# One-hot tables of a top-2 expert router built with the batch's columns innermost, and read by the tensor engine in strides of eight elements

## The reference

```python
var = mean(x * x, axis=-1)
xn = rms_w * (x * rsqrt(var + 1e-6))
gate = xn @ wg_W + wg_b + (cond @ gg_W + gg_b)
cw = top-2 weights of softmax(gate), zero for the other six experts
h1 = relu(x @ W1[e] + b1[e])
h2 = relu(h1 @ W2[e] + b2[e])
out = x + sum over e of cw[e] * (h2 @ W3[e] + b3[e])
```

## Time and profile before

| | |
|---|---|
| runs of the kernel before, us | 550.54, 550.29, 549.07; median 550.29 |
| profiled execution, its own time | 554.03 us |
| its span, first to last instruction | 552.3 us |
| mean granted clock of PE | 0.925 |
| busy share: PE, weight load, DVE, ACT, POOL | 88%, 76%, 60%, 55%, 53% |
| chain that ended last, by engine | PE 73%, DVE 9%, POOL 8%, issue 4%, ACT 3% |
| chain, DVE's lines L771 and L774 | 2% and 1% |

### The profile page before, as it was taken

The page is one execution under the profiler, slowest core; times in us unless marked ns, Lnnn a source line. Parts: engine busy times, 40 slices in busy tenths (PEclk is TensorE's granted clock), DMA queues, the critical chain, the costliest instruction groups (busy, mean ns, idle before and its releaser), DMA issues.

```text
span 552.3 us, 13779 instructions
## 1 busy us (share of the span) xinstructions
PE 486.5 (88%) x4218; PEld 420.4 (76%) x4219; DVE 332.6 (60%) x599; ACT 303.2 (55%) x616; POOL 294.9 (53%) x395
## 2 busy tenths in 40 slices
PE   7942544997989799999999999999999999999982
PEld 4521533786878588988988898889888989898871
DVE  4678994696896455655564555556645655565540
ACT  7999812475759345544554454545455544554440
POOL 3300156058777766656664656566656655664442
PEclk9985555898899899999999999999999999999996
DMA  8999116111332133322222223222222322433000
GB/s 319 426 418 392 49 23 221 63 21 33 54 105 41 27 59 53 52 49 38 43 49 47 42 41 53 47 41 43 57 38 40 52 52 38 53 48 48 3 2 0
DMA packets 19976, 45.30 MB, mean 82 GB/s; under 512 B 4971, under 2 KB 14253, under 8 KB 17773
## 3 DMA queue, kind: packets, MB, share of 16 engines
q0 software_dynamic: 14976, 18.64, 20.2%
q1 hardware_dynamic: 4896, 26.26, 12.3%
q10 hardware_dynamic: 77, 0.04, 0.0%
HBM read 36.52 MB, written 14.42 MB: 92 GB/s over the span
## 4 chain that ended last, share of the span: by engine, by line
PE 73%; DVE 9%; POOL 8%; issue 4%; ACT 3%; DMA 1%; POOLq 0%; ACTq 0%; DVEq 0%
PE bank L962 50%; PE bank L985 16%; POOL out L445 3%; PE bank L880 3%; PE bank L946 3%; DVE area L771 2%; POOL area L432 2%; DVE area L774 1%; PE bank L870 1%; DMA area<-in_x,tab_from 1%; POOL bound L390 1%; ACT area L585 1%; DVE area L815 1%; ACT unread_late L530 1%; ACT w_hi L549 1%
## 5 line engine op out<-in xcount | busy, mean ns | idle before, releaser
L962 PE MATMUL bank<-area,w_hi 128*128 128x256 f16 x1872 | 316.7, 277 | 11.7 <-DVE area L815 8.5
L962 PE MATMUL bank<-area,w_lo 128*128 128x256 f16 x936 | 258.7, 276 | 0.0
L585 ACT ACTIVATE area<-bank,cprm 128x256 f32<-128x256 f32 x312 | 158.7, 560 | 124.6 <-PE bank L962 111.3
L962 PEld LDWEIGHTS bank<-area,w_hi 128*128 x1872 | 185.0, 99 | 37.3 <-issue 13.8
L813 DVE CAST area<-area 128x512 f16<-128x512 f32 x156 | 72.2, 463 | 164.2 <-ACT area L585 160.8
L445 POOL DMA_INDIRECT out<-area,cto x78 | 128.3, 1644 | 48.1 <-issue 34.2
L985 PE MATMUL bank<-w_hi,area 128*128 x624 | 110.2, 275 | 3.7 <-DVE area L815 3.7
L815 DVE TENSOR_TENSOR area<-area 128x512 f16<-128x512 f32 x156 | 108.2, 694 | 5.4
L962 PEld LDWEIGHTS bank<-area,w_lo 128*128 x936 | 93.0, 99 | 11.9
L432 POOL DMA_INDIRECT area<-in_x,cfrom x72 | 78.0, 1083 | 42.6 <-POOL cfrom L427 31.6
L985 PE MATMUL bank<-w_lo,area 128*128 x312 | 85.9, 275 | 0.0
(11 more groups left out here) (155 smaller groups left out, 352.2 us busy)
## 6 DMA issues: line engine op xcount, KB each, us to landing
stage<-in_weights SPq DMA_DIRECT2D x7, 1024.0 KB, 10.3
w_lo<-in_weights SPq DMA_DIRECT2D x6, 1024.0 KB, 23.2
area<-in_x SPq DMA_DIRECT2D x8, 512.0 KB, 7.5
out<-in_x SPq DMA_DIRECT2D x8, 512.0 KB, 12.4
w_hi<-in_weights SPq DMA_DIRECT2D x3, 1024.0 KB, 25.9
out<-area,cto POOLq DMA_INDIRECT x78
area<-in_x,cfrom POOLq DMA_INDIRECT x72
prm<-in_b SPq DMA_DIRECT2D x1, 1024.0 KB, 15.5
```

The source lines that it names most:

```text
L585: act.activation(to[:, m * T:(m + 1) * T], ps_h[layer][b][:, a * T:(a + 1) * T], ACT.Relu, bias=cprm[:, slot, 4 + 4 * layer + m:5 + 4 * la ...
L962: ins = nc.tensor.matmul(banks[m // 2][:, (m % 2) * T:(m % 2 + 1) * T], wp[:, bass.ds(w + at_w, P)], xp[:, cols], start=(k == 0 and n == 0 ...
```

## The change

The three tables of stage two and the constants they are compared with get the eight columns of a batch as their innermost dimension. `iota_r` becomes 256 x 8 (each number eight times), `iota_c` 39 x 8; `values` is stored value by value in place of pair by pair. The place of a pair is kept as fp16 (`row16`) in place of fp32. The eight compares of L771 become one two-input operation on 128 x 2048 fp16 elements; `hot_c` and `hot_q` keep their 312 and 936 elements, but every operand now runs along the batch's columns in steps of one element. The matmul reads the same numbers: column n of a batch is now 128 weights and 117 moving columns that lie eight elements (16 bytes) apart. The bigger `iota_r` lies in the part of `w_lo` that is expert 1's, which nothing writes before the low parts of chunk 2, after stage two. Number and shape of the matmuls, all waits and their order stay as they were.

```diff
--- before.py
+++ after.py
@@ -108,8 +108,7 @@
 
         behind = sb("behind", [P, P], F16)
         ones16 = sb("ones16", [P, P], F16)
-        iota_r = sb("iota_r", [P, T], F16)
-        iota_c = sb("iota_c", [P, TILES], F16)
+        iota_c = sb("iota_c", [P, TILES, BATCH], F16)
         packed = sb("packed", [P, KH + KH * E + 2 * E * KM], F32)
         rmsw = packed[:, 0:KH]
         wg_in = packed[:, KH:KH + KH * E].rearrange("p (k e) -> p k e", k=KH)
@@ -134,7 +133,7 @@
         halves = sb("halves", [P, J], F32)
         restart = sb("restart", [P, E * J], F32)
 
-        values = sb("values", [P, 2 * J, 3], F16)
+        values = sb("values", [P, 3, 2 * J], F16)
         rms_tmp = sb("rms_tmp", [P, J], F32)[:, :]
         rank = sb("rank", [P, E], F32)
         small = sb("small", [P, 7, 16], F32)
@@ -181,11 +180,12 @@
         wt = take(2 * J)
         wt_h = take(2 * J)
         code, pad, pos_f, wsum = (take(COLS).rearrange("p (u t) -> p u t", u=SUB) for _ in range(4))
-        tile16, row_f = take(J).bitcast(F16), take(2 * J)
+        tile16, row16 = (take(J).bitcast(F16) for _ in range(2))
+        take(J)
         pairs = area[:, at[0]:at[0] + 2 * E * J]
-        hot_c = take(BATCH * TILES).bitcast(F16).rearrange("p (r n c) -> p r n c", r=2, n=BATCH)
-        hot_r = take(BATCH * T).bitcast(F16).rearrange("p (r n c) -> p r n c", r=2, n=BATCH)
-        hot_q = take(3 * BATCH * TILES).bitcast(F16).rearrange("p (r n v c) -> p r n v c", r=2, n=BATCH, v=3)
+        hot_c = take(BATCH * TILES).bitcast(F16).rearrange("p (r c n) -> p r c n", r=2, n=BATCH)
+        hot_r = take(BATCH * T).bitcast(F16).rearrange("p (r c n) -> p r c n", r=2, n=BATCH)
+        hot_q = take(3 * BATCH * TILES).bitcast(F16).rearrange("p (r v c n) -> p r v c n", r=2, n=BATCH, v=3)
         assert at[0] <= J * H
 
         def unread(first, n):
@@ -200,6 +200,8 @@
         xT = w_hi[:, E * WE - XT * 4 * 2 * P:].bitcast(F32).rearrange("p (r c) -> p r c", r=XT)
 
         gates_t = w_lo[0:E, 0:WE].bitcast(F32).rearrange("p (r c) -> p r c", r=4)
+
+        iota_r = w_lo[:, WE:WE + T * BATCH].rearrange("p (c n) -> p c n", n=BATCH)
 
         def staged(q):
 
@@ -353,9 +355,9 @@
 
             pool.affine_select(out=behind[:, :], in_=behind[:, :], compare_op=ALU.is_gt, fill=-1.0,
                                base=0, pattern=[[1, P]], channel_multiplier=-1).then_inc(s_const, 1)
-            pool.iota(iota_r[:, :], pattern=[[1, T]], base=0, channel_multiplier=0,
+            pool.iota(iota_r, pattern=[[1, T], [0, BATCH]], base=0, channel_multiplier=0,
                       allow_small_or_imprecise_dtypes=True).then_inc(s_const, 1)
-            pool.iota(iota_c[:, :], pattern=[[1, TILES]], base=0, channel_multiplier=0,
+            pool.iota(iota_c[:, :, :], pattern=[[1, TILES], [0, BATCH]], base=0, channel_multiplier=0,
                       allow_small_or_imprecise_dtypes=True).then_inc(s_const, 1)
             pool.iota(rank[:, :], pattern=[[-1, E]], base=E, channel_multiplier=0,
                       allow_small_or_imprecise_dtypes=True).then_inc(s_const, 1)
@@ -653,7 +655,7 @@
 
             link(dve.tensor_scalar(tokv[P // 2:P, :], tokv[P // 2:P, :], 1.0, None, ALU.add))
             for k in range(2):
-                dve.tensor_copy(values[:, k * J:(k + 1) * J, 0], tokv[:, :])
+                dve.tensor_copy(values[:, 0, k * J:(k + 1) * J], tokv[:, :])
 
             def small_inputs():
 
@@ -752,28 +754,27 @@
             link(dve.tensor_copy(slot_i, slot_f))
             dve.tensor_scalar(part_i, slot_i, T - 1, None, ALU.bitwise_and)
             link(dve.tensor_scalar(slot_i, slot_i, T.bit_length() - 1, None, ALU.logical_shift_right))
-            dve.tensor_copy(row_f, part_i)
+            dve.tensor_copy(row16, part_i)
             link(dve.tensor_copy(tile16, slot_i))
             dve.wait_ge(s_exp, 1)
             link(dve.tensor_reduce(rs, je(ex[:, 0:E * J]), AX.X, ALU.add))
             link(dve.reciprocal(rs, rs))
             link(dve.tensor_scalar(wt[:, 0:J], rs, WSCALE, None, ALU.mult))
             link(dve.tensor_tensor(wt[:, J:2 * J], ex[:, E * J:], wt[:, 0:J], ALU.mult))
-            link(dve.tensor_copy(values[:, :, 1], wt))
-            link(dve.tensor_copy(wt_h, values[:, :, 1]))
-            link(dve.tensor_tensor(values[:, :, 2], wt, wt_h, ALU.subtract))
+            link(dve.tensor_copy(values[:, 1, :], wt))
+            link(dve.tensor_copy(wt_h, values[:, 1, :]))
+            link(dve.tensor_tensor(values[:, 2, :], wt, wt_h, ALU.subtract))
             for b in range(2 * J // BATCH):
                 ns = slice(b * BATCH, (b + 1) * BATCH)
                 if b >= 2:
                     dve.wait_ge(s_inv, b - 1)
-                for n in range(BATCH):
-                    at_n = b * BATCH + n
-                    dve.tensor_scalar(hot_r[:, b % 2, n, :], iota_r[:, :], row_f[:, at_n:at_n + 1], None, ALU.is_equal)
-                link(dve.tensor_tensor(hot_c[:, b % 2], iota_c[:, :].unsqueeze(1).to_broadcast([P, BATCH, TILES]),
-                                       tile16[:, ns].unsqueeze(2).to_broadcast([P, BATCH, TILES]), ALU.is_equal))
+                dve.tensor_tensor(hot_r[:, b % 2], iota_r, row16[:, ns].unsqueeze(1).to_broadcast([P, T, BATCH]),
+                                  ALU.is_equal)
+                link(dve.tensor_tensor(hot_c[:, b % 2], iota_c[:, :, :],
+                                       tile16[:, ns].unsqueeze(1).to_broadcast([P, TILES, BATCH]), ALU.is_equal))
                 ins = dve.tensor_tensor(hot_q[:, b % 2],
-                                        hot_c[:, b % 2].unsqueeze(2).to_broadcast([P, BATCH, 3, TILES]),
-                                        values[:, ns, :].unsqueeze(3).to_broadcast([P, BATCH, 3, TILES]), ALU.mult)
+                                        hot_c[:, b % 2].unsqueeze(1).to_broadcast([P, 3, TILES, BATCH]),
+                                        values[:, :, ns].unsqueeze(2).to_broadcast([P, 3, TILES, BATCH]), ALU.mult)
                 ins.then_inc(s_hot, 1)
 
             link(dve.tensor_tensor(cmp_t.rearrange("p (i e) -> p i e", e=E),
@@ -929,8 +930,8 @@
                 pe.wait_ge(s_hot, b + 1)
                 for n in range(BATCH):
                     for u in range(SUB):
-                        ins = nc.tensor.matmul(ps_slots[:, u, :], hot_r[:, b % 2, n, u * P:(u + 1) * P],
-                                               hot_q[:, b % 2, n].rearrange("p v c -> p (v c)"),
+                        ins = nc.tensor.matmul(ps_slots[:, u, :], hot_r[:, b % 2, u * P:(u + 1) * P, n],
+                                               hot_q[:, b % 2, :, :, n].rearrange("p v c -> p (v c)"),
                                                start=(b == 0 and n == 0 and u == 0),
                                                stop=(b == 2 * J // BATCH - 1 and n == BATCH - 1 and u == SUB - 1))
                 ins.then_inc(s_inv, 1)
```

## The result

The changed kernel takes 558.5 us (median of 4 runs, 558.12 to 558.99) against 550.31 for the kernel before (median of 4): a ratio of 1.0138, with a 95% interval of 1.011 to 1.0165. It is 8.2 us slower, where 7 us faster was forecast.

What follows compares the result with a forecast made beforehand. DVE was taken to bound stage two's eight batches. Start +0.6 and tables saving 8.6 gave -7.7 us at `tab_from`, -7.0 at L946 after POOL's gating: 550.29 - 7.0 = 543.3, say 543.5 us, range 541.5 to 546.0.

Steps and rivals of the forecast that it cites:

- The tables on DVE: Stage two's one-hot tables: 0.53 ns per element, a batch 2.06 us in place of 3.13, eight save 8.6 us.
- The bound of 1.06 ns per element: DVE's tables: slower limit for two-input operations, taken from L772 and L774; the forecast took 0.53 ns.
- the second rival: DVE's tables get no faster per element: hot_r 2.31 us, a batch 3.79, total 556.2 us; chance 0.04.
- 1.76 us for 16 matmuls is under 2.06, if a column read 16 bytes from the last costs what an adjacent one does: PE's one-hot matmuls in stage two: spread columns cost nothing extra, so DVE still bounds; tab_from and s_from -7.7 us.
- The first rival: PE reads spread columns, weights or moving, at half rate: 195 ns a matmul, 3.12 us a batch; chances 0.18 and 0.08.
- its slow form: Half-rate PE reads in stage two without a clock rise: 3.12 us a batch, L787 +1.8 us, 552.1 us; chance 0.18.
- the form where the clock rises: Half-rate PE reads, but gapless work raises the clock to 2.4 GHz: gain mostly returns, 545 to 547 us; chance 0.08.
- The start, +0.6 us: Bigger iota_r and iota_c: DVE's first real instruction 1.6 us later, partly hidden, so batch 0 starts 0.6 us later.
- the bound of twice that rate: GpSimd's iota with an inner step of zero: upper limit of 2.2 us at the start; 0.6 us was taken.
- What is late next: After the tables, POOL's parameters gate the gathers: first gather -2.6 to -7.7 us, L946 taken as -7.0 us.
- The third rival: At the gathers: POOL's lateness passes on whole, landing 8.97 us after the first gather, -2.6 us, 547.7 us; chance 0.17.
- That `parameters` would take 7.36 us again: POOL's parameters before the gathers: start about 65.7 us, duration 7.36 us as before, end at 73.1 us.

Runs made afterwards that it cites:

- the strided kernels: Changed kernel, iotas behind the other constants, new layout kept only for hot_r (weights): 550.57 us; or only for hot_c, hot_q, values (moving columns): 553.9 us.
- quiet iotas: Changed kernel with the two eightfold iotas moved after the inverse_rms loop (22 to 24 us), where DVE copies from PSUM: 554.06 us, 1.0059 of before.
- the mixed layout: Against the changed kernel with quiet iotas: hot_r stays in batches of eight, hot_c and hot_q in two groups of four; 543.14 and 543.37 us.

## Why the prediction was wrong

- **The tables on DVE**: right. 1.23, 0.32 and 0.65 us were measured where 1.23, 0.31 and 0.64 were forecast, and 2.06 us a batch. The bound of 1.06 ns per element, and with it the second rival, was wrong.
- **"1.76 us for 16 matmuls is under 2.06, if a column read 16 bytes from the last costs what an adjacent one does"**: this step failed, and with it the sum. A batch takes PE 3.43 us. The first rival had the mechanism, and the strided kernels show which of its two operands it is: the moving columns. Its own price was short: 214 ns measured against 195, which over the 127 that count is 2.4 us. The Trainium skill, "SBUF — State Buffer", in the section on the DMA port swizzle, names lines of 16 bytes and a penalty for each access to a new one; with that penalty the runs with moving columns agree (107 ns with two in a line, 208 and 214 with one). The same note reads as if a step of 8 elements of 16 bits were still free; that step is the one of the changed kernel, it cost 214 ns in place of 97.5, and the measurement decides. The note doesn't tell weights from moving columns; here the weights cost 2 ns a matmul. I had given this rival 0.18 in its slow form and 0.08 in the form where the clock rises; the clock never rose on its own in these reads, and would not have helped. My argument against the rival, that PE asks for less per time at 1.2 GHz, was the mistake: 0.83 ns per column is already faster than the 1.8 ns at which such reads come.
- **The start, +0.6 us**: this term was sized too low by 3.7. The rate of GpSimd's iota was 0.78 ns per element in the rows of before, but (3.76 - 0.66) / (2048 - 312) = 1.79 ns with an inner step of zero, a little over the bound of twice that rate. That makes 3.9 us for the first instruction and 2.8 for the first copy. Then a thing I had not counted: PE's first tiles ran slowly (1.95 us for eight transposes in place of 1.07), which made 4.3. The forecast has no term for it. It came in every profile with an early big iota, but also in one of the two of the kernel before, so that it isn't shown that the late copies bring it on. The size is that of one pair of executions: the four profiles with the full iota early have their first batch at 54.34 to 55.11, and those of before at 50.11 and 52.06. The times agree with it, 4.3 to 4.7 us between the changed kernel and the one with quiet iotas.
- **What is late next**: not reached in the changed kernel, where GpSimd waited 8.83 us for `s_from` after its parameters. In the mixed layout it is reached and costs nothing. The landing of the gathers kept its distance from the first issue, 7.2 to 7.6 us in all profiles but the first of before. The third rival assumed such a fixed distance, but GpSimd never held the gathers back, so its price was not tested. That `parameters` would take 7.36 us again was wrong: they took 4.6 to 5.9 us in the ten profiles whose `hot_c` and `hot_q` are built the new way. They took 7.3 and 7.4 in the two of before and 8.7 with strided weights only, where these two tables are built as before. With strided moving columns DVE still has its eight short instructions for `hot_r`, and the parameters took 4.6: the time goes with the form of the two small tables, not with the number of DVE's instructions.
- **The sum of what was measured**: +4.3 at the start and +3.5 in stage two (30.54 - 27.07) are 7.8 us at L788, and the medians differ by 8.2. The forecast had +0.6 and -8.3 in their place. The mixed layout, with neither cost and DVE at 2.13 us a batch, is at -7.2 us: the forecast's size was that of a kernel that reads its moving columns closer.

## What to carry to other kernels

Before a layout is turned so that one engine reads it fast, the other engine's read has to be priced too, and the operand matters: on PE a step of 16 bytes doubled the time of moving columns and left weights nearly alone (at 1.2 GHz), and a step of 8 bytes cost a tenth, so a turned table that PE reads as moving columns is better cut into groups of four fp16 columns than of eight. A constant that grows eightfold isn't free because nothing waits for it: GpSimd's iota held up two of DVE's instructions from SBUF to SBUF while it ran and none of its copies from PSUM, so it belongs beside those. And PE's busy share rises when its operands come slowly; the count of matmuls per microsecond doesn't.

## What the hardware did that I had not expected

- Moving columns that lie 16 bytes apart come at 1.8 ns each at both levels of the clock, 1.2 and 2.4 GHz, and the clock fell from 1.00 to 0.50 while PE was shown busy with them from 52.5 us on. Over 27 us of such matmuls in the changed kernel the clock stayed at 0.50.
- A DVE instruction of 32 elements took 3.62 us beside an iota on GpSimd, from its start to the iota's end.
- GpSimd's iota costs 0.78 ns per element with steps of one and 1.79 with an innermost dimension of eight at a step of zero.
- One kernel's first batch comes up to 2 us earlier or later from one execution to another (50.11 and 52.06 before; 50.07 to 51.98 with the quiet iotas), while stage two repeats to 0.1 us. The late ones have slow rows of PE near 8 us (1.95 us for eight transposes in place of 1.07). What brings these on was not tried; the recorded clock was 1.00 in four of the seven profiles that have them.
